# Five input buffers in place of two in the first stage of an attention and FFN block, their loads issued early

## The chip, the cores and the metric

The kernel runs on one core of one Trainium2 chip. The metric is the device time of one execution in microseconds (us). The engines are TensorE (PE), VectorE (DVE), ScalarE (ACT), GpSimd (POOL) and SyncE (SP), which here only issues DMAs.

## What is computed

A transformer block on x of 2 x 2048 x 256 (f32), with adaptive layer norms: a small conditioning vector c gives six modulations, and attention and a mixture of low-rank experts are added to x behind gates.

```python
mod = (_silu(L0_c) @ L0_wmod).reshape(L0_c.shape[0], 6, 1, -1)
sa, ca, ga, sb, cb, gb = (mod[:, 0], mod[:, 1], mod[:, 2], mod[:, 3], mod[:, 4], mod[:, 5])
...
h = _layernorm(x, axis=-1) * (1 + ca) + sa
x = x + ga * _L0_attn_ref(h, L0_attn_W_qkv, L0_attn_b_qkv, L0_attn_W_out, L0_attn_b_out)
h = _layernorm(x, axis=-1) * (1 + cb) + sb
x = x + gb * _L0_ffn_ref(h, ...)
```

The attention is causal, with 16 heads of 16. Inside it, the part that matters here is its beginning:

```python
qkv = x @ W_qkv.T + b_qkv
q, k, v = jnp.split(qkv, 3, axis=2)
```

## The kernel before

The 4096 rows of x (two sequences of 2048) are taken as 8 blocks of 512 (`NBLK`), each as 4 tiles of 128 rows. There are three stages. The first makes q, k and v of every block. The second is the attention, 8 groups of heads over 4 blocks of queries each. The third projects the result and does the FFN. Products are done in three passes of a high and a low half (`PASSES`, `product`), so each operand is split in two.

The first stage, for block n:

- SP loads the block into one of two buffers, `xs[:, n % 2]` (`load_x`, L429 to 431). Before it issues load n it waits until block n-2 has been rescaled by DVE (`xhat_done` at n-1), since that frees the buffer.
- DVE waits for the load and takes mean and variance (`moments`, L1191, which calls `statistics`, L409 to 412), ACT takes the root (`root`, L1058), and DVE writes `xhat` (`rescale`, L1195, which calls `standardise`, L416 to 423).
- PE turns `xhat` with 8 transposes (`turn`, L756, instructions at L761). ACT applies the modulation and makes the high half of `hT`, DVE the low half (`modulate`, L1062; `low`, L1198).
- PE projects q and k, 4 pieces of 6 matmuls of 512 columns (`project_qk`, L765, in `product` at L391), then v, 24 matmuls of 256 columns (`project_v`, L775).
- ACT moves the pieces of q and k to `parts[:, n % 2]` (`high`, L1072). Before it does, it waits until the stores of block n-2 out of the same buffer have landed (`parts_stored`). DVE makes the low half (`qk_low`, L1210). DVE moves v to `v_nat` (`v_rows`, L1217).
- SP stores `parts` to `qk_parts` in device memory, 4 DMAs of 512 KB (`store_parts`, L433 to 439), and from the round of block 1 on reads a block of the first head group back from there into `kst` and `qst`, 12 DMAs of 64 KB (`load_stacks`, L441 to 454).

The order on each engine is written out by hand. PE does, for n from 1 on, the turn of block n+1, then q and k and v of block n (L799 to 803). The q and k of block n wait until the low half of block n+1 is there and until DVE has taken the same piece of block n-1 out of PSUM (L767, L771). DVE does in round n: moments and rescale of block n+2, the low half of n+1, the four pieces of n, `v_nat` of n (L1251 to 1258). ACT does in round n: modulation of n+1, root of n+2, the pieces of n (L1090 to 1095). SP's loop, which the change touches, is L473 to 478:

```python
                load_x(2)
                for n in range(NBLK):
                    if n + 3 < NBLK:
                        load_x(n + 3)
                    store_parts(n)
                    if 1 <= n <= NJ:
                        load_stacks(0, n - 1)
```

SP executes this strictly in order. So load n+3 is issued after all of round n-1's stores and stack loads.

The attention's first work on PE is a fill of `ps` for the row maxima (`fill`, L832, matmuls at L863), which waits until `v_nat` of block 7 is written (`v_out`, L915). DVE reduces it to `mx` (L1266, L1270). POOL and ACT go on to the attention when all stores of `parts` have landed too (`first_stage_over`, L372): POOL then clears and fills `vw` (L633, L641), ACT does the exponentials (L1121).

Of the kernel before, what the change touches and what calls it, by code (L numbers as in the profile page):

```python
# [5 lines left out]
P = 128  # L6
# [7 lines left out]
B, S, D = 2, 2048, 256  # L14
# [7 lines left out]
KC, FC = D // P, FF // P  # L22
T = B * S
BLK = 512
TT = BLK // P
NBLK = T // BLK
# [19 lines left out]
LAST_OF_G = {g: max(LAST[u] for u in range(NU) if UNITS[u][0] == g) for g in range(NG)}  # L46
UNIT_AT_END = {LAST[u]: u for u in range(NU)}
PV_LAG, P_BUFS = 2, 4


def skip_of(n):
# [124 lines left out]
def until(eng, sem, count):  # L176
    if count > 0:
        eng.wait_ge(sem, count)


def build_program(nc, x, cT, wmod, wqkvT, bqkv, bv, woutT, bout, w1, b1, ar1, bl1, w2, b2, ar2, bl2, out):
# [4 lines left out]
    with ExitStack() as whole:  # L186
        def sem(name):
            return whole.enter_context(nc.semaphore(name))
# [4 lines left out]
        class Region:  # L193
# [50 lines left out]
        a = Region(rest_at)  # L244
# [12 lines left out]
        ar1_sb = a("ar1_sb", [P, KC, ZP])  # L257
        bl1_sb = a("bl1_sb", [LR, FF])
        bl2_sb = a("bl2_sb", [LR, D])
        xs = a("xs", [P, 2, TT, D])  # L260
        xhat = a("xhat", [P, TT, D])
        hf = a("hf", [P, KC, BLK])
        hT = a.pair("hT", [P, 2, KC, BLK])
# [1 line left out]
        stats = a("stats", [P, TT, 6])  # L265
        mv = a("mv", [P, TT, 2])
        rstd = a("rstd", [P, TT])
# [19 lines left out]
        f = Region(v_at)  # L287
# [10 lines left out]
        f = Region(bufs_at)  # L298
# [15 lines left out]
        xb_in = x.rearrange("(n t p) d -> n p t d", t=TT, p=P)  # L314
# [3 lines left out]


        c_in, wmod_in, wqkv_in, bias_in = sem("c_in"), sem("wmod_in"), sem("wqkv_in"), sem("bias_in")  # L320
        small_in, pad_in, x_in = sem("small_in"), sem("pad_in"), [sem(f"x_in{q}") for q in range(2)]
        consts, tables, padded, exp_c, silu_done = sem("consts"), sem("tables"), sem("padded"), sem("exp_c"), sem("silu_done")
        setup, w_hi, w_lo = sem("setup"), sem("w_hi"), sem("w_lo")
        small_hi, small_lo = sem("small_hi"), sem("small_lo")
# [2 lines left out]
        dve1, var_done, std_done, xhat_done, xT_done = (  # L327
            sem("dve1"), sem("var_done"), sem("std_done"), sem("xhat_done"), sem("xT_done"))
# [78 lines left out]
        def statistics(dve, link, xs, stats, mv, var_done):  # L407
            for t in range(TT):
                link(dve.bn_stats(stats[:, t, :], xs[:, t, :]), wait=(t == TT - 1))  # L409
            for t in range(TT - 1):  # L410
                link(dve.bn_aggr(mv[:, t, :], stats[:, t, :]), wait=False)
            dve.bn_aggr(mv[:, TT - 1, :], stats[:, TT - 1, :]).then_inc(var_done, 1)

        def standardise(dve, link, i, xs, mv, rstd, xhat, std_done, xhat_done, turned):
            until(dve, std_done, i + 1)
            link(dve.reciprocal(rstd[:], rstd[:]))  # L416
            until(dve, *turned)
            for t in range(TT):
                last = dve.tensor_scalar(xhat[:, t, :], xs[:, t, :], mv[:, t, 0:1], rstd[:, t:t + 1],  # L419
                                         ALU.subtract, ALU.mult)  # L420
                if t < TT - 1:
                    link(last, wait=False)
            last.then_inc(xhat_done, 1)

        with nc.Block() as block:
            @block.sync
            def _(sp):

                def load_x(n):  # L429
                    until(sp, xhat_done, n - 1)  # L430
                    sp.dma_start(xs[:, n % 2], xb_in[n]).then_inc(x_in[n % 2], 16)

                def store_parts(n):  # L433
                    for t in range(2):
                        sp.wait_ge(qk_lo, n * 2 * KC + (t + 1) * KC)
                        for h in range(2):
                            dst = qk_parts[t, h, :, n * BLK:(n + 1) * BLK]
                            sp.dma_start(dst.rearrange("(c p) t -> p c t", p=P),
                                         parts[:, n % 2, h, t * KC:(t + 1) * KC, :].bitcast(F32)).then_inc(parts_stored[n % 2], 16)

                def load_stacks(g, J, parts_of_load=ALL_PARTS):  # L441
                    c, hg, q = g // HG, g % HG, g % 2
                    n = c * NJ + J
                    sp.wait_ge(parts_stored[n % 2], 16 * 4 * (n // 2 + 1))
                    sp.wait_ge(ones_set[q], CLEARS)
                    cols = slice(n * BLK, (n + 1) * BLK)
                    for t, par in parts_of_load:
                        stack, order = (qst[q], (0, 0, 1)) if t == 0 else (kst[q], (0, 1, 0))
                        for row, h in enumerate(order):
                            src = qk_parts[t, h, hg * GH * HD:(hg + 1) * GH * HD, cols].rearrange(  # L450
                                "(p two r) t -> two r p t", two=2, r=HD)
                            at = par * STACK + row * HD
                            sp.dma_start(stack[at:at + HD, :, J * BLK:(J + 1) * BLK].bitcast(F32),  # L453
                                         src[par]).then_inc(kq_in[q][J], 16)

                sp.dma_start(c_sb[:], cT.rearrange("(k p) b -> p k b", p=P)).then_inc(c_in, 16)
                load_x(0)
                sp.dma_start(wmod_sb[:], wmod.rearrange("(k p) n -> p k n", p=P)).then_inc(wmod_in, 16)
                sp.dma_start(wqkv_sb[:], wqkvT.rearrange("(k p) n -> p k n", p=P)).then_inc(wqkv_in, 16)
                sp.dma_start(bq_sb[:], bqkv).then_inc(bias_in, 16)  # L460
                sp.dma_start(bv_sb[:], bv.broadcast_to((P, D))).then_inc(bias_in, 16)
                load_x(1)
                sp.dma_start(wout_sb[:], woutT.rearrange("(k p) n -> p k n", p=P)).then_inc(small_in, 16)
                sp.dma_start(b1_sb[:], b1).then_inc(small_in, 16)
# [4 lines left out]
                for r0 in (0, 32, 64):  # L469
                    sp.dma_start(bl1_sb[r0:r0 + ER], bl1).then_inc(pad_in, 16)  # L470
                    sp.dma_start(bl2_sb[r0:r0 + ER], bl2).then_inc(pad_in, 16)
                load_x(2)
                for n in range(NBLK):  # L473
                    if n + 3 < NBLK:
                        load_x(n + 3)
                    store_parts(n)
                    if 1 <= n <= NJ:
                        load_stacks(0, n - 1)
# [98 lines left out]
            def _(pool):  # L577
# [67 lines left out]
                def split_w(k):  # L645
                    pool.wait_ge(w_in, 16 * 3 * (k + 1))
                    width = KC * FF // W_PIECES
                    pieces = [(w1_p[0][:].rearrange("p k f -> p (k f)")[:, k * width:(k + 1) * width],
                               w1_p[1][:].rearrange("p k f -> p (k f)")[:, k * width:(k + 1) * width], w1_in[:]),
                              (w2_p[0][:, k, :], w2_p[1][:, k, :], w2_in[:])]  # L650
                    for hi, _, full in pieces:
                        pool.tensor_copy(hi, full).then_inc(ffn_hi, 1)
                    pool.wait_ge(ffn_hi, 2 * (k + 1))
                    for hi, lo, full in pieces:
                        pool.tensor_tensor(lo, full, hi.bitcast(F32), ALU.subtract).then_inc(ffn_lo, 1)
# [79 lines left out]
            def _(pe):  # L735
# [96 lines left out]
                def fill(e):  # L832
# [13 lines left out]
                    if ev[0] == "turn_x":  # L846
# [5 lines left out]
                        last.then_inc(fill_done, 1)  # L852
                        return
                    _, u, r, pairs, cb, width, on_diagonal = ev
                    g, J = UNITS[u]
                    q, k = qst[g % 2], kst[g % 2]
# [329 lines left out]
            def _(dve):  # L1186

                ready = Links(dve, setup)
                link1 = Links(dve, dve1)

                def moments(n):  # L1191
                    dve.wait_ge(x_in[n % 2], (n // 2 + 1) * 16)
                    statistics(dve, link1, xs[:, n % 2], stats, mv, var_done)

                def rescale(n):  # L1195
                    standardise(dve, link1, n, xs[:, n % 2], mv, rstd, xhat, std_done, xhat_done, (xT_done, n * KC))

                def low(n):  # L1198
                    dve.wait_ge(h_out, (n + 1) * 2 * KC)
# [44 lines left out]
                dve.wait_ge(bias_in, 32)  # L1244
                ready(dve.tensor_scalar(bq_sb[:, 0:KC], bq_sb[:, 0:KC], QSCALE, None, ALU.mult))
                moments(1)
                low(0)
                rescale(1)
# [12 lines left out]
                def maxima(e, ev):  # L1261
                    _, u, r, pairs, cb, width, _ = ev
                    bank = S_BANK + 2 * (e % 2)
                    dve.wait_ge(fill_done, e + 1)
                    if len(pairs) == 2:
                        dve.tensor_reduce(mx[:, u % 2, :, :, r, cb],  # L1266
                                          ps[:, bank:bank + 2, 0:2 * width].rearrange("p a (h x) -> p a h x", h=2),
                                          AX, ALU.max).then_inc(max_red, 1)
                    else:
                        dve.tensor_reduce(mx[:, u % 2, :, pairs[0], r, cb], ps[:, bank:bank + 2, 0:width],  # L1270
                                          AX, ALU.max).then_inc(max_red, 1)
# [223 lines left out]
```

## Time and profile before

| | us |
|---|---|
| median of 3 runs | 1308.25 |
| lowest and highest run | 1307.49, 1309.97 |
| the profiled execution's own time | 1304.39 |
| its span, first to last instruction | 1302.4 |
| PE busy | 1218.0 (94%) |
| DVE busy | 933.2 (72%) |
| ACT busy | 800.5 (61%) |
| POOL busy | 178.0 (14%) |
| mean granted clock of PE, share of full speed | 0.965 |

All rows further down are of the one profiled execution. Its times count from the start of the span. "L391" is line 391 of the kernel. An entry in brackets, as [4.50 <-DMA xs<-in_x], tells how long the engine was idle just before, and what ended it. SPq rows are issues of DMAs by the queue SP, and the time is that of the issuing, not of the transfer. PE's matmuls overlap, so their starts tell the pace, and not their durations. The first stage takes the first 109.77 us of the span, the attention most of the rest.

### The profile page before, as it was taken

To read this page: it belongs to the slowest core of one execution; us is meant where nothing else is said; L and a number is where in the kernel's file an instruction comes from. 1 tells how busy PE (TensorE), PEld (TensorE's weight loads), DVE (VectorE), ACT (ScalarE), POOL (GpSimd) and SP (SyncE) were. 2 spreads that over 40 slices of the span, in tenths; PEclk is the share of its full clock that TensorE was granted. 3 is DMA by queue.
4 is the path that set the end of the run, shared out by engine and by line. 5 is a ranking of instruction groups with operands and counts; after the bars stand their busy time and mean duration, and the time that the engine had idled before them with its cause. 6 is when DMAs were issued, how large, how long until landed. Compare 5 with 4: busy or idle time off the path is not lost.

```text
span 1302.4 us, 24602 instructions
## 1 busy us (share of the span) xinstructions
PE 1218.0 (94%) x9928; PEld 723.5 (56%) x9928; DVE 933.2 (72%) x1247; ACT 800.5 (61%) x1611; POOL 178.0 (14%) x153
## 2 busy tenths in 40 slices
PE   6988789999999999999999999999998899999997
PEld 5875334444444444444444444444444788898886
DVE  5877897888787887778887778786631576766553
ACT  4451466777777776767777667777675554444442
POOL 5205600000211000000000000200110132222310
PEclk9987798999999999999999999999899999999999
DMA  5793120031032021013003003500000222111100
GB/s 170 247 289 144 52 64 10 8 87 34 27 108 70 10 65 54 3 45 98 10 13 90 19 10 93 138 10 10 3 10 27 50 65 65 53 38 50 57 17 33
DMA packets 58121, 79.58 MB, mean 61 GB/s; under 512 B 12680, under 2 KB 28752, under 8 KB 58008
## 3 DMA queue, kind: packets, MB, share of 16 engines
q1 hardware_dynamic: 58008, 78.01, 20.3%
q8 instruction: 78, 1.28, 0.4%
q14 instruction: 35, 0.29, 0.1%
HBM read 47.57 MB, written 29.62 MB: 59 GB/s over the span
## 4 chain that ended last, share of the span: by engine, by line
PE 67%; DVE 12%; ACT 9%; issue 8%; SPq 2%; DMA 1%; POOL 0%; POOLq 0%; ACTq 0%; DVEq 0%
PE ps L907 21%; PE ps L882 17%; PE ps L863 9%; PE ps L391 8%; ACT prob L1121 7%; PE ps L1008 5%; DVE mx L1270 5%; PE ps L820 4%; PE ps L811 2%; DVE xhat L419 1%; DVE hid_lo L1413 1%; SPq L453 1%; ACT o_sb L1106 1%; DVE stats L409 1%; DMA wqkv_sb<-in_wqkvT 1%
## 5 line engine op out<-in xcount | busy, mean ns | idle before, releaser
L1121 ACT ACTIVATE prob<-ps 128x512 f32<-128x512 f32 (+3 forms) x1280 | 598.1, 537 | 263.0 <-PE ps L820 161.3
L1270 DVE TENSOR_REDUCE mx<-ps 128x2 f32<-128x1024 f32 (+1 forms) x512 | 594.0, 1188 | 148.2 <-PE ps L863 85.5
L882 PE MATMUL ps<-qst,kst 64*128 64x512 f32 (+3 forms) x1280 | 387.0, 446 | 18.9 <-ACT prob L1121 14.3
L882 PEld LDWEIGHTS ps<-qst,kst 64*128 64x128 f32 x1280 | 183.9, 188 | 270.2 <-ACT prob L1121 211.3
L907 PE MATMUL ps<-prob,vw 128*32 128x512 f32 (+3 forms) x3032 | 317.8, 492 | 3.4 <-ACT o_sb L1106 3.4
L863 PE MATMUL ps<-kst,qst 62*128 62x512 f32 (+3 forms) x1280 | 288.7, 425 | 21.5 <-DVE mx L1270 18.1
L863 PEld LDWEIGHTS ps<-kst,qst 62*128 62x128 f32 x1280 | 137.1, 193 | 95.4 <-DVE mx L1270 51.5
L907 PEld LDWEIGHTS ps<-prob,vw 128*32 128x32 f32 x3032 | 60.5, 108 | 86.9 <-issue 38.7
L820 PE MATMUL ps<-mask_kh,eye_h 64*128 64x128 bf16 x1024 | 99.6, 225 | 0.0
L1266 DVE TENSOR_REDUCE mx<-ps 128x4 f32<-128x512 f32 x64 | 60.9, 955 | 30.8 <-PE ps L811 30.4
L1413 DVE TENSOR_TENSOR hid_lo<-hidf,hid_hi 128x512 fp32r<-128x512 f32 x64 | 68.0, 1095 | 20.7 <-ACT hid_hi L1161 20.6
L1008 PE MATMUL ps<-w_hi,hid_hi 128*128 128x284 f32 x256 | 74.5, 315 | 5.3 <-ACT hid_hi L1161 5.3
L811 PE MATMUL ps<-mask_qh,eye_h 64*128 64x128 bf16 x1024 | 74.4, 225 | 0.0
L641 POOL COPY vw<-v_nat 128x1024 f32<-128x1024 f32 x8 | 8.3, 1039 | 469.3 <-PE ps L907 469.2
L1008 PE MATMUL ps<-w_lo,hid_hi 128*128 128x284 f32 x256 | 72.1, 306 | 0.0
L1161 ACT ACTIVATE hidf<-ps,b_sb 128x512 f32<-128x512 f32 x64 | 43.9, 686 | 37.7 <-PE ps L997 37.7
L1008 PEld LDWEIGHTS ps<-w_hi,hid_hi 128*128 128x128 f32 x256 | 51.0, 199 | 8.7 <-ACT hid_hi L1161 8.3
L391 PE MATMUL ps<-hT_hi,w_hi 128*128 128x512 f32 x128 | 52.4, 409 | 1.1 <-ACT hid_hi L1161 1.1
L820 PEld LDWEIGHTS ps<-mask_kh,eye_h 64*128 64x128 bf16 x1024 | 42.6, 97 | 17.1 <-issue 5.8
L1008 PEld LDWEIGHTS ps<-w_lo,hid_hi 128*128 128x128 f32 x256 | 51.3, 200 | 0.4
L1144 ACT ACTIVATE gexp<-gexp 128x12 f32<-128x12 f32 x16 | 3.4, 212 | 78.2 <-DVE gexp L1383 78.2
L391 PE MATMUL ps<-hT_hi,w_lo 128*128 128x512 f32 x128 | 50.9, 398 | 0.0
(157 smaller groups left out, 1350.5 us busy)
## 6 DMA issues: line engine op xcount, KB each, us to landing
qk_parts<-parts SPq DMA_DIRECT2D x32, 512.0 KB, 5.4
qst<-qk_parts SPq DMA_DIRECT2D x192, 64.0 KB, 2.4
kst<-qk_parts SPq DMA_DIRECT2D x192, 64.0 KB, 2.4
xs<-in_x SPq DMA_DIRECT2D x16, 512.0 KB, 8.4
o_all<-o_sb SPq DMA_DIRECT2D x32, 256.0 KB
o_raw<-o_all SPq DMA_DIRECT2D x16, 256.0 KB
rd<-rden_rows SPq DMA_DIRECT2D x16, 256.0 KB
out<-y SPq DMA_DIRECT2D x8, 512.0 KB, 3.2
```

The lines of the kernel that those rows point to most:

```text
L391: last = pe.matmul(out, lhs(i, k), rhs(j, k), start=(start and k == 0 and n == 0), stop=(stop and k == chunks - 1 and n == len(PASSES) - 1))
L811: last = pe.matmul(ps[:, bank + par, col:col + P], eye_h[rows, half, :], mask_qh[rows, half, :], start=False, stop=True, skip_group_check= ...
L820: last = pe.matmul(ps[:, L_BANK + (4 * n + h) % L_BUFS, 0:P], eye_h[rows, half, :], mask_kh[rows, half, :], start=False, stop=True, skip_g ...
L863: last = pe.matmul(ps[:, bank + par, at * width:(at + 1) * width], q[rows, p, J * BLK + r * P:J * BLK + (r + 1) * P], k[rows, p, cb * BLK: ...
L882: last = pe.matmul(ps[:, L_BANK + (4 * n + h) % L_BUFS, 0:BLK - skip], kst[g % 2][rows, h // 2, t * P:(t + 1) * P], qst[g % 2][rows, h // ...
L907: last = pe.matmul(ps[32 * h:32 * h + 32, O_BANK, skip + lo:skip + hi], vw[:, g % 2, t, h, :], prob[:, n % P_BUFS, h, lo:hi], start=(t == ...
L1008: last = pe.matmul(ps[:, Y_BANK + t, 0:D + ZP], hid[u][:, m, t * P:(t + 1) * P], w2_p[v][:, m, :], start=(e == 0), stop=(e == len(order) - 1))
L1121: act.activation(prob[:, n % P_BUFS, h, 0:width], ps[:, L_BANK + i % L_BUFS, 0:width], ACT.Exp).then_inc(exp_done, 1)
L1161: act.activation(dst, ps[:, H_BANK + m % 2, :], ACT.Relu, bias=b1_sb[:, m:m + 1]).then_inc(f1_out, 1)
L1266: dve.tensor_reduce(mx[:, u % 2, :, :, r, cb], ps[:, bank:bank + 2, 0:2 * width].rearrange("p a (h x) -> p a h x", h=2), AX, ALU.max).then ...
L1270: dve.tensor_reduce(mx[:, u % 2, :, pairs[0], r, cb], ps[:, bank:bank + 2, 0:width], AX, ALU.max).then_inc(max_red, 1)
L1413: dve.tensor_tensor(hid[1][:, m, :], hidf[:, m % HRING, :], hid[0][:, m, :].bitcast(F32), ALU.subtract).then_inc(hid_lo_done, 1)
```

## The change

`xs` gets five buffers instead of two, with a semaphore each. Load n waits until block n-5 has been rescaled. SP issues loads 2, 3 and 4 behind the small weights, where load 2 was alone, and in its loop load n+5 in place of load n+3: load 5 in round 0, load 6 in round 1, load 7 in round 2. Nothing is computed in another way, and the number of DMAs is the same.

```diff
+X_BUFS = 5
...
-        xs = a("xs", [P, 2, TT, D])
+        xs = a("xs", [P, X_BUFS, TT, D])
...
-        small_in, pad_in, x_in = sem("small_in"), sem("pad_in"), [sem(f"x_in{q}") for q in range(2)]
+        small_in, pad_in, x_in = sem("small_in"), sem("pad_in"), [sem(f"x_in{q}") for q in range(X_BUFS)]
...
                 def load_x(n):
-                    until(sp, xhat_done, n - 1)
-                    sp.dma_start(xs[:, n % 2], xb_in[n]).then_inc(x_in[n % 2], 16)
+                    until(sp, xhat_done, n - X_BUFS + 1)
+                    sp.dma_start(xs[:, n % X_BUFS], xb_in[n]).then_inc(x_in[n % X_BUFS], 16)
...
-                load_x(2)
+                for n in range(2, X_BUFS):
+                    load_x(n)
                 for n in range(NBLK):
-                    if n + 3 < NBLK:
-                        load_x(n + 3)
+                    if n + X_BUFS < NBLK:
+                        load_x(n + X_BUFS)
                     store_parts(n)
...
                 def moments(n):
-                    dve.wait_ge(x_in[n % 2], (n // 2 + 1) * 16)
-                    statistics(dve, link1, xs[:, n % 2], stats, mv, var_done)
+                    dve.wait_ge(x_in[n % X_BUFS], (n // X_BUFS + 1) * 16)
+                    statistics(dve, link1, xs[:, n % X_BUFS], stats, mv, var_done)
 
                 def rescale(n):
-                    standardise(dve, link1, n, xs[:, n % 2], mv, rstd, xhat, std_done, xhat_done, (xT_done, n * KC))
+                    standardise(dve, link1, n, xs[:, n % X_BUFS], mv, rstd, xhat, std_done, xhat_done, (xT_done, n * KC))
```

## Rows read from the trace of the kernel before

**Rows 1.** Windows: length; busy us of PE, PEld, DVE, ACT, POOL; clock; DMA share; GB/s.
```profile
60.00:70.00 10.00, 7.50 (x47) 6.43 (x47) 8.25 (x19) 5.40 (x9) 0.00 (x0) 1.00 1.01 289
...
80.00:90.00 10.00, 10.00 (x45) 8.38 (x44) 5.94 (x17) 3.66 (x7) 0.00 (x0) 0.74 0.98 304
```

**Rows 2.** Waits, 0 to 125 us, DVE: total us, times, longest.
```profile
DVE stats L409 <- DMA xs<-in_x: 13.5, 5, 4.5
```

**Rows 3.** Timeline of DVE: start, duration, line, operation, count, idle before.
```profile
47.78 1.39 DVE L409 BATCH_NORM_STATS2 stats<-xs 128x6 f32<-128x256 f32 x4
...
55.23 1.22 DVE L1219 TENSOR_TENSOR v_nat<-ps,bv_sb 128x1024 f32<-128x1024 f32 x1
60.95 1.40 DVE L409 BATCH_NORM_STATS2 stats<-xs 128x6 f32<-128x256 f32 x4 [4.50 <-DMA xs<-in_x]
```

**Rows 4.** Timeline of PE: turns (L761), first and last matmuls (L391), first fill (L863).
```profile
44.25 1.03 PE L761 MATMUL ps<-ident,xhat 128*128 128x128 f32 x8
...
53.58 1.03 PE L761 MATMUL ps<-ident,xhat 128*128 128x128 f32 x8
...
64.78 1.09 PE L761 MATMUL ps<-ident,xhat 128*128 128x128 f32 x8 [1.71 <-DVE xhat L419]
...
77.14 1.09 PE L761 MATMUL ps<-ident,xhat 128*128 128x128 f32 x8 [1.77 <-DVE xhat L419]
79.02 0.76 PE L391 MATMUL ps<-hT_hi,wqkv_hi 128*128 128x512 f32 x1 [0.79 <-DVE parts L1213]
...
85.41 0.39 PE L391 MATMUL ps<-hT_hi,wqkv_hi 128*128 128x512 f32 x1
...
90.35 1.03 PE L761 MATMUL ps<-ident,xhat 128*128 128x128 f32 x8
...
99.82 0.40 PE L391 MATMUL ps<-hT_hi,wqkv_hi 128*128 128x512 f32 x1
...
105.43 0.28 PE L391 MATMUL ps<-wqkv_hi,hT_hi 128*128 128x256 f32 x1
...
109.77 0.44 PE L863 MATMUL ps<-kst,qst 62*128 62x128 f32 x4 [1.36 <-issue]
```

**Rows 5.** Timeline of the queue SP: issues of stores, loads and stack loads.
```profile
34.22 2.88 SPq L438 DMA_DIRECT2D qk_parts<-parts  x4
...
56.42 0.42 SPq L431 DMA_DIRECT2D xs<-in_x  x1
...
67.81 0.42 SPq L431 DMA_DIRECT2D xs<-in_x  x1
...
79.09 0.41 SPq L431 DMA_DIRECT2D xs<-in_x  x1
...
86.46 2.75 SPq L453 DMA_DIRECT2D kst<-qk_parts  x6
```

**Rows 6.** Windows (columns as in Rows 1), cut where the kind of transfer changes.
```profile
18.00:34.00 16.00, 14.80 (x65) 12.28 (x66) 9.95 (x22) 6.35 (x11) 13.68 (x15) 1.00 0.13 39
...
60.80:66.20 5.40, 3.37 (x28) 2.93 (x26) 4.82 (x15) 2.84 (x6) 0.00 (x0) 1.00 1.05 391
66.20:72.50 6.30, 5.83 (x26) 4.76 (x27) 3.43 (x5) 2.56 (x4) 0.00 (x0) 1.00 0.92 181
...
90.60:93.50 2.90, 2.90 (x17) 2.34 (x16) 2.90 (x5) 2.52 (x4) 0.00 (x0) 1.00 0.82 169
```

**Rows 7.** Timelines of ACT and of POOL.
```profile
87.67 2.40 ACT L1076 ACTIVATE parts<-ps,bq_sb 128x512 fp32r<-128x512 f32 x4
...
126.83 1.28 ACT L1121 ACT_TABLE_LOAD   x1 [20.51 <-PE ps L820]
...
111.58 1.81 POOL L633 MEMSET vw<- 128x2048 f32 x1 [68.78 <-DMA qk_parts<-parts]
```

**Rows 8.** Window (columns as in Rows 1) in which the clock is at half.
```profile
113.00:130.00 17.00, 12.94 (x77) 7.04 (x73) 15.01 (x18) 2.63 (x4) 16.01 (x18) 0.51 0.01 2
```

**Rows 9.** The page: granted clock in tenths, 40 slices of 32.6 us.
```profile
PEclk9987798999999999999999999999899999999999
```

## The prediction

> **What bounds the kernel now.** First the busy table by stretch, for the stage that the change touches [rows 1]: from 60 to 70 us TensorE (PE) is busy for 7.50 of 10 us, its clock falls to a mean of 0.74 in 80 to 90, and the DMA engines are busy at 0.98 to 1.01 of their time in both. Three things could set the pace, and the shares don't say which. Next the waits of VectorE (DVE) [rows 2]: 13.5 us in 5 pieces for `xs`. The timelines put this in order. DVE's statistics of block 5 start at 60.95, after 4.50 us of waiting for the load; those of blocks 6 and 7 are two more such rows, with 3.66 and 3.62 us [rows 3]. PE follows: its turns of blocks 5 and 6 start after waits of 1.71 and 1.77 us for `xhat`, and the projection behind the second waits 0.79 us more (a like row stands behind the first) [rows 4]. The queue SP shows why the loads are late: load 5 is issued at 56.42, load 6 at 67.81, load 7 at 79.09 [rows 5]. Each comes behind the stores and the 12 small stack loads of the round before. It is not a taken buffer that holds them: load 5 needs block 3 rescaled, and by 47.78 DVE is already at the statistics of block 4 [rows 3].
>
> How fast would PE go without these waits? Turns at 44.25 and 53.58 give 9.33 us a block [rows 4]. DVE's own block of work, from 47.78 to the end of `v_nat` at 56.45, is 8.67 us, less than that [rows 3]. From the turn at 53.58 the next ones come after 11.20, 12.36 and 13.21 us, and the last block's first matmul (it has no turn) 9.47 us after that, where 9.33 each is possible: 1.87 + 3.03 + 3.88 + 0.14 = 8.92 us [rows 4]. Of the 3.88, most is the clock. Fifteen matmuls of 512 columns fill 79.02 to 85.41, 0.426 us each (the 1.2 GHz level); the last block's 24 fill 99.82 to 105.43, 0.234 each (2.4 GHz). That is 15 x 0.192 = 2.9 us [rows 4]. What PE did before this fall were the waits just named.
>
> **The change, part by part.** (a) Loads 2 to 5 are now issued one behind the other, where load 2 was. All small transfers are issued ahead of them as before, SP has nothing else until the first store at 34.22 [rows 5], and the DMA engines are busy at 0.13 from 18 to 34 us [rows 6]. The three loads that come forward, 0.52 MB each, take 1.3 us each at the 391 GB/s of a full stretch [rows 6]. Cost: 0, since that idle time hides them; without it 3.9 us, on whatever small load came behind, and none does. (b) Load 6 takes the place that load 4 had, right after the first store, load 7 that of load 5, 56.42. DVE will ask for block 7 at about 74, so all three late waits (4.50 + 3.66 + 3.62 = 11.8 us) go. They don't count in full: PE is next, and only its 8.92 count. Until 56.42 no wait changes, so the saving begins there. (c) SP loses the issues at 67.81 and 79.09, 0.42 us each [rows 5]. (d) The loads' waits for `xhat` look back further and are met when SP comes to them; more semaphores and a larger tile add no instruction: 0.
>
> What is late next? With PE at 9.33 us a block, the projections of blocks 4 to 7 begin at 63.7, 73.0, 82.4 and 91.0. PE ends its last block 8.9 us before the 108.41 of now, at 99.5, and the attention's first fill, which waits for the last `v_nat` (1.36 us), comes at 100.9 instead of 109.77 [rows 4]. DVE keeps up, by its 8.67. The other that must is the queue: `parts` has two buffers, so ScalarE (ACT) writes block n+2 only when the store of block n has landed. SP's rounds begin at 56.42, 67.81 and 79.09, 11.39 and 11.28 us apart, longer than 9.33 [rows 5]. Unhindered, six stack loads are issued in 2.75 us [rows 5], 0.46 each, so a round of 17 issues is about 8 us of SP's own; the rest is waiting for room in the DMA queues. These need 5.4 us for a store, 6.3 for stacks and an input load, and 2.9 for stacks alone where all were queued in time [rows 6]. Taking the load away gives between 1.3 us (its bytes at 391 GB/s) and 3.4 (6.3 less 2.9). So a round of 11.3 becomes 7.9 to 10.0 us if the DMA engines pace it, and 10.9 if SP's issuing does. The store of block 2 is through at about 66.2 [rows 6]; that of block 5, for which ACT's last block waits, at 66.2 + 3 rounds. Behind it come 2.4 us of ACT [rows 7] and 0.7 of DVE, and then `v_nat`. That meets PE's 99.5 at a round of 10.0. I take 9.8, nearest to the measured 11.3 less the load's bytes: hidden, by half a microsecond. At 10.9 the stage ends 2.8 us later.
>
> Behind the stage, GpSimd clears `vw` when the last store has landed, at 111.58, for 1.81 us, and ACT's first work of the attention is at 126.83 [rows 7]. The store shifts less than PE, by some 5 to 8 us, and this cover of 13 us shrinks by up to 4 and stays. All later stages do the same work in the same order, so they shift whole.
>
> One rule speaks against the change. In 60 to 90 us the DMA share is about 1.0 [rows 1]. The Trainium skill (Perfetto Trace Analysis, "What "DMA-bound" means") says that where the DMA engines or the issuing sequencer bind, large descriptors are what matters; loading ahead only moves bytes. By it the rounds keep their pace, which is the first rival below.
>
> **The sum.** 1.87 + 3.03 + 3.88 + 0.14 = 8.9 us. The profiled run took 1304.39 us (span 1302.4) and becomes 1295.5. The median of the three runs, 1308.25, is 3.86 above the profiled one; with the saving taken from the median: 1299.3.
>
> **The rivals.**
> First, the queue takes the place of the load. For it: rounds of 11.3 us at a DMA share near 1.0. Against it: 3 us of a round is waiting for room, which the removed bytes give back. At a round of 10.9 the stage ends 2.8 us later than forecast, 6.1 saved: 1302.2.
>
> Second, the clock. If its fall inside the stage comes anyway, the 2.9 us stay: 1302.2. For it: the rows don't say what starts a fall, and another lasts from 113 to 130 [rows 8]. Against it: none is there up to 78, where PE has hardly a gap, and after the change it has none to 99. The other way, if 113 to 130 were spent less at half clock, PE's 12.94 busy us there could shrink [rows 8], of which DVE lets pass a part; I allow 3 us. The Trainium skill (TensorE: Matmul & The Clock Gate, "HAM oscillation") reckons the loss as throttled time times a half: 3.2 us for the 6.4 seen, where the starts of the matmuls give 2.9.
>
> Third, the gain is swallowed before the end: the attention starts on the last store, by `vw`, and not on `v_nat`. Against it: 13 us of cover. It gives 1306 to 1309.
>
> Fourth, slower. All of the attention now starts 8.9 us earlier against the clock's changes, and a fall can come where PE sets the pace. From 163 us on the page's clock is at 9 tenths nearly throughout [rows 9]; a microsecond at half clock there costs half a microsecond. It takes (8.9 + 2.6) x 2 = 23 us more of it before the kernel is slower by 0.2%; the longest in the rows is 17 [rows 8]. With 30 us more: 1299.3 + 15 = 1314.
>
> **How the numbers follow.** Forecast, 8 to 9.5 us saved, and with it what the clock may give beyond: 0.62. Queue 0.15, clock fall kept 0.10, swallowed 0.09, slower 0.04. 0.2%, 2.6 us, is about what a measurement of this kernel can tell from no change. Faster: 0.62 + 0.15 + 0.10 = 0.87; same 0.09; slower 0.04. The range runs from 3 us of clock beyond the forecast, with the 0.8 by which the lowest run lies under the median, to the queue's and the clock's 1302.2 with the 1.7 of the highest above it: 1295.5 to 1304.
>
> **What would show it.** Right: no wait of DVE for `xs` after block 1, turns 9.33 us apart from 44 us on, full clock to 99, the first fill near 100.9, SP's rounds under 10 us. The queue rival: ACT's pieces of `parts` waiting for the stores of two blocks before, and `v_nat` waiting for them. The clock rival: a stretch at half clock before 100. Swallowed: ACT's first work of the attention not 9 us earlier. The prediction is wrong if the first fill comes at 101 and the span is not 9 us shorter; the loss would then lie behind the stage.

## The result

| | before | after |
|---|---|---|
| median of 6 runs, us | 1307.3 (1305.43 to 1309.97) | 1299.57 (1295.65 to 1302.93) |
| the profiled execution's own time | 1304.39 | 1297.24 |
| its span | 1302.4 | 1295.3 |
| its first fill of the attention | 109.77 | 103.36 |

The ratio of after to before is 0.994, interval 0.9922 to 0.9958, or 5.5 to 10.2 us saved. A later measurement of the same kernel, `after_again` below, gives 0.9944 (0.9922 to 0.9966). The forecast was 1299.3. A ratio is the time of a kernel over that of the kernel before, measured beside it; the numbers in brackets behind a ratio are its 95% interval, those behind a median in the table the lowest and the highest run.

The forecast named the stage's end as the place where the saving is made, and there it was too large: the first fill came 6.4 us earlier, not 8.9. What it said of the loads and of PE came out. What it said of the queue did not, and the queue rival is what happened. (A round is one pass of SP's loop: a store of `parts` in four DMAs, and 12 stack loads.) First the engines between 60 and 90 us, in the columns of [rows 1]:

```profile
60.00:70.00 10.00, 10.00 (x63) 8.85 (x62) 9.56 (x22) 6.20 (x11) 0.00 (x0) 1.00 0.96 308
70.00:80.00 10.00, 10.00 (x64) 8.90 (x63) 9.55 (x23) 5.88 (x10) 0.00 (x0) 1.00 0.84 273
80.00:90.00 10.00, 10.00 (x64) 8.89 (x63) 6.47 (x9) 5.23 (x8) 0.00 (x0) 1.00 0.87 285
```

PE is busy for all of it at full clock. Before, it was busy for 7.50 of the first 10 us, and its clock was 0.74 in the last 10 [rows 1]. The statistics of blocks 5 to 7 follow one another without any wait for a load, where the first of them waited 4.50 us [rows 3]. DVE's timeline:

```profile
56.60 1.39 DVE L410 BATCH_NORM_STATS2 stats<-xs 128x6 f32<-128x256 f32 x4
...
65.19 1.39 DVE L410 BATCH_NORM_STATS2 stats<-xs 128x6 f32<-128x256 f32 x4
...
73.79 1.39 DVE L410 BATCH_NORM_STATS2 stats<-xs 128x6 f32<-128x256 f32 x4
...
99.40 2.73 DVE L1215 SCALAR_TENSOR_TENSOR parts<-ps,bq_sb,parts 128x512 fp32r<-128x512 f32 x4 [6.96 <-ACT parts L1078]
102.04 1.22 DVE L1221 TENSOR_TENSOR v_nat<-ps,bv_sb 128x1024 f32<-128x1024 f32 x1
```

The last two lines are the new thing: DVE stands 6.96 us for ACT before the last block, and its last `v_nat` starts at 102.04. PE's timeline (turns, first fill), against [rows 4], and ACT's:

```profile
62.99 1.03 PE L763 MATMUL ps<-ident,xhat 128*128 128x128 f32 x8
...
72.33 1.03 PE L763 MATMUL ps<-ident,xhat 128*128 128x128 f32 x8
...
81.66 1.03 PE L763 MATMUL ps<-ident,xhat 128*128 128x128 f32 x8
...
103.36 0.69 PE L865 MATMUL ps<-kst,qst 62*128 62x128 f32 x4 [3.75 <-issue]
```
```profile
86.59 2.45 ACT L1078 ACTIVATE parts<-ps,bq_sb 128x512 fp32r<-128x512 f32 x4 [1.50 <-DMA qk_parts<-parts]
98.68 2.42 ACT L1078 ACTIVATE parts<-ps,bq_sb 128x512 fp32r<-128x512 f32 x4 [9.64 <-DMA qk_parts<-parts]
121.29 1.28 ACT L1123 ACT_TABLE_LOAD   x1 [20.19 <-PE ps L822]
```

The turns are 9.34 and 9.33 us apart. PE ends its projections at 103.36 - 3.75 = 99.61; forecast was 99.5. Then it stands 3.75 us in place of 1.36. It waits for the last `v_nat`; DVE writes that behind its pieces of `parts`, those come behind ACT's, and ACT waited 9.64 us for the store of block 5 to land. The reason is in SP's rounds, to be compared with [rows 5]:

```profile
57.06 3.90 SPq L439 DMA_DIRECT2D qk_parts<-parts  x4
61.06 4.28 SPq L454 DMA_DIRECT2D qst<-qk_parts  x6
65.38 2.75 SPq L454 DMA_DIRECT2D kst<-qk_parts  x6
68.18 3.06 SPq L439 DMA_DIRECT2D qk_parts<-parts  x4
71.34 5.12 SPq L454 DMA_DIRECT2D qst<-qk_parts  x6
76.51 3.02 SPq L454 DMA_DIRECT2D kst<-qk_parts  x6
79.57 3.11 SPq L439 DMA_DIRECT2D qk_parts<-parts  x4
...
89.80 13.91 SPq L439 DMA_DIRECT2D qk_parts<-parts  x12
```

From store to store the rounds take 11.12, 11.39 and 10.23 us, against 11.39 and 11.28 before. In the second there is no input load any more, and it is not shorter. Windows of the same execution show why a load's bytes were no cost there (columns as in [rows 1]):

```profile
60.00:66.00 6.00, 6.00 (x44) 5.54 (x43) 6.00 (x11) 3.43 (x6) 0.00 (x0) 1.00 1.06 399
66.00:68.00 2.00, 2.00 (x10) 1.63 (x9) 1.56 (x9) 1.38 (x4) 0.00 (x0) 1.00 0.70 131
76.00:80.00 4.00, 4.00 (x23) 3.43 (x22) 3.96 (x9) 2.48 (x4) 0.00 (x0) 1.00 0.59 134
```

While stores run, the window has 399 GB/s; while stack loads run, 131 to 134 GB/s with the DMA engines 0.59 to 0.70 busy. SP issues six stack loads of 64 KB in 2.75 us, 0.46 us each, which is 142 GB/s: in these stretches it is SP's issuing that sets the rate, and the DMA engines had room for an input load.

### The profile page after: what moved, and what is told of

Its sections match the earlier page's. It is cut to its first block, busy times and chain, and to the rows that moved or that the text cites. A ratio compares the mean times of both kernels' runs of the same rounds, so it can differ in the third digit from the quotient of the medians.

```text
span 1295.3 us, 24602 instructions
## 1 busy us (share of the span) xinstructions
PE 1216.4 (94%) x9928; PEld 725.0 (56%) x9928; DVE 931.2 (72%) x1247; ACT 800.0 (62%) x1611; POOL 178.1 (14%) x153
## 4 chain that ended last, share of the span: by engine, by line
PE 72%; DVE 10%; ACT 9%; issue 8%; DMA 1%; POOL 0%; SPq 0%; POOLq 0%; ACTq 0%; DVEq 0%
PE ps L909 21%; PE ps L884 17%; PE ps L392 11%; PE ps L865 9%; ACT prob L1123 7%; PE ps L1010 5%; DVE mx L1272 5%; PE ps L822 4%; PE ps L813 2%; DVE hid_lo L1415 1%; ACT o_sb L1108 1%; DMA wqkv_sb<-in_wqkvT 1%; DVE stats L410 1%; DVE xhat L420 1%; DVE x L1320 1%
```

## The experiments

Each kernel was timed beside the kernel before the change. Its profile is of one execution.

**Buffers or place.** Two kernels take the change apart. The first has the five buffers and leaves the issues where they were:

```diff
-                for n in range(2, X_BUFS):
-                    load_x(n)
+                load_x(2)
                 for n in range(NBLK):
-                    if n + X_BUFS < NBLK:
-                        load_x(n + X_BUFS)
+                    if n + 3 < NBLK:
+                        load_x(n + 3)
```

> Five buffers, but load n+3 issued in round n as before the change. If the place of the issue is what counts: DVE waits 4.50, 3.66 and 3.62 us for blocks 5 to 7 as before, the first fill comes near 109.8 us and the time is that of before (1307) within 2 us. If the waits for a free buffer counted: those waits go, first fill near 103.4, and the time is that of the changed kernel (about 1299.6).

Ratio 1.0011 (0.9993 to 1.0028). DVE's waits for `xs` from 36 to 112 us (total, times, longest) and the first fill:

```profile
DVE stats L410 <- DMA xs<-in_x: 11.5, 3, 4.3
```
```profile
109.80 0.44 PE L864 MATMUL ps<-kst,qst 62*128 62x128 f32 x4 [1.36 <-issue]
```

The second is the kernel before with its two buffers, and each load one round earlier:

```diff
                 load_x(2)
+                load_x(3)
                 for n in range(NBLK):
-                    if n + 3 < NBLK:
-                        load_x(n + 3)
+                    if n + 4 < NBLK:
+                        load_x(n + 4)
```

> Two buffers as before, load n+4 issued in round n (loads 2 and 3 ahead of the loop), so loads 5, 6 and 7 go out at about 43, 56.4 and 68 us. If the place of the issue counts: no wait of DVE above 1 us after block 1 (block 7's load lands near 73.5, DVE asks at 73.8), first fill near 103.4, time as the changed kernel's, about 1300. If the number of buffers counted: waits of 3 us or more for blocks 5 to 7, and about 1305 to 1307.

Ratio 0.9955 (0.9939 to 0.9971), median 1300.75. The first fill, and ACT's waits for stores in the stage:

```profile
102.85 0.44 PE L864 MATMUL ps<-kst,qst 62*128 62x128 f32 x4 [3.42 <-issue]
```
```profile
ACT parts L1077 <- DMA qk_parts<-parts: 14.5, 3, 8.1
```

So three more buffers alone give nothing, and the earlier place with two buffers gives the whole effect within the measurement. The extra buffers only allow a freer choice of place, and the kernel needs one round.

**What held the stage's end.** The changed kernel with a third buffer of `parts`, laid over the input weights, which are used up when block 2 needs it (the cut shows the count, ACT's wait and ACT's write; SP's and DVE's uses go with them):

```diff
+PART_BUFS = 3
...
-                    until(act, parts_stored[n % 2], n // 2 * 16 * 4)
+                    until(act, parts_stored[n % PART_BUFS], n // PART_BUFS * 16 * 4)
...
-                        act.activation(parts[:, n % 2, 0, c, :], ps[:, QK_BANK + c, :], ACT.Identity,
+                        act.activation(part(n)[0][:, part(n)[1], 0, c, :], ps[:, QK_BANK + c, :], ACT.Identity,
```

> The changed kernel with three buffers of parts (the third lies over weights that are used up), so ACT waits for the store of block n-3 instead of n-2. In the changed kernel ACT's last block waited 9.64 us for a store and the first fill 3.75 us behind PE. If that wait costs what the stage lost against the forecast: ACT's last block starts near 92.5, the last v_nat is done near 100.8, first fill near 101, 2.4 us earlier than the changed kernel; time about 1297. If something else held v_nat (DVE's own work, or PE): first fill stays at 103.4 and the time at 1299.6.

```profile
100.65 0.44 PE L872 MATMUL ps<-kst,qst 62*128 62x128 f32 x4 [1.36 <-issue]
```

The first fill is at 100.65, where the forecast had 100.9, and the wait before it is the old 1.36. SP's rounds are as long as before (stores at 56.74, 68.06, 79.47, 89.83). So the two buffers of `parts` passed the length of the rounds on, and that cost 2.7 us at the stage's end. The median is 1299.7, ratio 0.9943 (0.9921 to 0.9965): the 2.7 us don't show in it. More on this below.

The same third buffer in the kernel before:

> The kernel before the change with three buffers of parts. If the stores held nothing up before the change: DVE still waits 11.8 us for blocks 5 to 7, first fill at 109.8, time that of before within 2 us. If the stores already cost something beside the loads: first fill 2 to 3 us earlier and 1304 to 1305.

```profile
DVE stats L416 <- DMA xs<-in_x: 12.9, 3, 4.6
```
```profile
111.92 0.33 PE L870 MATMUL ps<-kst,qst 62*128 62x128 f32 x2 [1.36 <-issue]
```

The waits are of 36 to 112 us. Ratio 1.0015 (0.9996 to 1.0034), so the third buffer gains nothing here: as long as the loads came late, the stores held nothing up. The fill is 2 us later than before. DVE's statistics of block 7 start at 86.74, 1.1 us later than before, and the profile has two falls of the clock in the stage, mean 0.79 in 64 to 72 and again in 88 to 96; whether the third buffer has a part in this stays open.

**What makes a round long.** The stack loads with a quarter of their bytes. This kernel leaves out three quarters of the first head group's q and k, so its results are not those of the reference; it serves for the first stage's timeline only:

```diff
+                    width = BLK // 4 if g == 0 else BLK
...
-                            sp.dma_start(stack[at:at + HD, :, J * BLK:(J + 1) * BLK].bitcast(F32),
-                                         src[par]).then_inc(kq_in[q][J], 16)
+                            sp.dma_start(stack[at:at + HD, :, J * BLK:J * BLK + width].bitcast(F32),
+                                         src[par, :, :, 0:width]).then_inc(kq_in[q][J], 16)
```

> The changed kernel, but the 48 stack loads of the first stage carry 128 columns each instead of 512 (the rest of the stacks is constants, so the attention of the first head group computes on part of its data only). Same number of issues, a quarter of their bytes (0.2 MB a round instead of 0.8). SP's rounds were 11.1 and 11.4 us in the changed kernel, though the input load was gone from the second. If a round is the drain of a store (5.4 us, in which SP stands still) and then SP's own issuing of the stack loads at 0.46 us each: rounds of 10.5 to 11.4 us, and ACT's last block still waits over 7 us for a store. If bytes set the round: under 10 us, and that wait is under 6 us.

It was executed once, which gives no ratio; two clearings of the stacks that it adds at the start make its whole stage some 3 us later. SP's timeline, and a window in which only stack loads run:

```profile
59.91 3.60 SPq L439 DMA_DIRECT2D qk_parts<-parts  x4
...
70.71 2.94 SPq L439 DMA_DIRECT2D qk_parts<-parts  x4
...
81.88 2.94 SPq L439 DMA_DIRECT2D qk_parts<-parts  x4
...
92.06 13.32 SPq L439 DMA_DIRECT2D qk_parts<-parts  x12
```
```profile
77.00:81.00 4.00, 4.00 (x19) 3.22 (x18) 3.54 (x14) 3.48 (x7) 0.00 (x0) 1.00 0.15 36
```

Rounds of 10.80, 11.17 and 10.18 us with 0.6 MB less in each, and ACT still waits 8.34 us. The DMA engines are busy for 0.15 of their time in that window, while SP issues one load after the other: behind the store it is SP's issuing alone that holds the round. The bytes alone don't make the round. Now the other way, the same bytes in fewer issues:

```diff
+WIDE = 2
...
-                    if 1 <= n <= NJ:
-                        load_stacks(0, n - 1)
+                    if 1 <= n <= NJ and n % WIDE == 0:
+                        load_first_stacks(n - WIDE)
```

> The changed kernel with the stack loads of the first stage taken for two blocks at once: 24 DMAs of 128 KB in place of 48 of 64 KB, the same bytes. If SP's issuing sets the pace of the stores: the store of block 5 is issued near 84 instead of 89.8, ACT's last block starts near 92.5 without a wait, first fill near 101 instead of 103.4, and the clearing of vw starts near 104 instead of 109.4; about 2 us less than the changed kernel, 1297 to 1298. If the bytes set it: the store of block 5 is still issued at 89 or later, first fill 103, time unchanged.

> As wide2, with all four blocks at once: 12 DMAs of 256 KB in the round of block 4. By SP's issuing: stores of blocks 2, 3 and 4 go out at once when DVE is done, near 55.5, 64 and 72.7; the 3.1 MB of stacks take some 8 us behind the store of block 4, so the store of block 5 lands near 93; first fill near 101 to 102, vw near 104. By bytes: the same bytes in one piece, first fill at 103 or later.

Neither half of what I expected of `wide2` came whole. The store of block 5 was indeed issued at 84.12, yet ACT waited 9.06 us for it, the first fill came at 102.79 and `vw` at 108.77, not 104. Ratio 0.9929 (0.9904 to 0.9955), which doesn't tell it from the changed kernel. Two windows in which its stack loads run:

```profile
66.00:70.00 4.00, 4.00 (x21) 3.32 (x20) 3.56 (x12) 2.77 (x6) 0.00 (x0) 1.00 1.07 138
84.00:88.00 4.00, 4.00 (x19) 3.22 (x18) 2.85 (x4) 2.95 (x5) 0.00 (x0) 1.00 1.04 166
```

Here the loads are all issued, the DMA engines are busy throughout, and they move 138 and 166 GB/s; why the second is faster stays open.

`wide4` is slower than the kernel before, 1.0037 (1.0011 to 1.0064), median 1312.12. A window of it while the stack loads run, and ACT:

```profile
80.00:98.00 18.00, 18.00 (x108) 15.82 (x107) 6.77 (x8) 5.32 (x8) 0.00 (x0) 1.00 1.02 129
```
```profile
107.08 2.42 ACT L1097 ACTIVATE parts<-ps,bq_sb 128x512 fp32r<-128x512 f32 x4 [19.09 <-DMA qk_parts<-parts]
```

All twelve loads, 3.1 MB, are issued by 80.37, and the store of block 5 right behind them. They pass at 129 GB/s for more than 18 us, and the store with them in front has to wait. My expectation of 8 us for them was off by a factor of three. Each of these loads writes 16 partitions, a store reads 128. That they are reads of device memory is not what makes them slow: input loads read it too and write 128 partitions, and from 18 to 21 us, where only they run, the changed kernel moves 383 GB/s. The Trainium skill (SBUF — State Buffer, "Door 1: The DMA port swizzle") says that the rate of a DMA follows from how many of 16 ports its partitions reach, and that 16 adjacent ones reach 4, 104 to 109 GB/s. The traces agree in kind, and measure more: 129 in `wide4`, 138 and 166 in `wide2`. No run here varies the number of partitions, so that it is the cause is argued, not shown.

So a block's stack loads cost SP 12 x 0.46 = 5.5 us of issuing, and the DMA engines between 0.79 MB / 166 GB/s = 4.7 us and 0.79 MB / 129 GB/s = 6.1 us (an estimate, by the rates of `wide2` and `wide4`). The two run side by side and are about equal, which is why taking away either leaves the round nearly as it is. A round is then roughly the drain of the store, 5.4 us, in which SP's issuing is slowed (the first ten issues of the round from 57.06 take 8.3 us, the last six 2.75), plus one of these.

> Three buffers of parts and the wide stack loads together. Both act on the same wait of ACT for a store, so together they give what one gives: first fill near 100.7, as with three buffers alone, and not 5 us less than the changed kernel. What is different from three buffers alone is only the end of the stores, vw near 104 instead of 109.1; if anything waits for that behind the stage it shows in the time, else about 1297 to 1299.

First fill 100.83, no wait of ACT for a store; ratio 0.9926 (0.9899 to 0.9953). As expected, the two act on one wait. The other half was wrong: `vw` comes at 109.30 and not near 104, so the stores don't end earlier.

**Out of the stores' way.** The changed kernel with the stack loads of blocks 2 and 3 behind the last store:

```diff
-                    if 1 <= n <= NJ:
+                    if 1 <= n <= NJ // 2:
                         load_stacks(0, n - 1)
+                for J in range(NJ // 2, NJ):
+                    load_stacks(0, J)
```

> The changed kernel with the stack loads of blocks 2 and 3 issued behind the last store instead of between the stores, still two buffers of parts. What stood between the stores in the queue was the stack loads, some 6 us a block by SP's issuing (0.46 us each) and as much by the DMA engines (131 GB/s into 16 partitions). So the stores of blocks 3 to 6 go out when DVE is done with them, ACT's last block starts near 92.4 without a wait, first fill 100.8, vw near 103.5 to 104. By the rival, that the drain of the stores alone holds ACT up: ACT's last block still waits and first fill stays above 102.

```profile
ACT parts L1080 <- DMA qk_parts<-parts: 0.6, 1, 0.6
```
```profile
101.14 0.44 PE L867 MATMUL ps<-kst,qst 62*128 62x128 f32 x4 [1.36 <-issue]
```
```profile
103.16 1.81 POOL L637 MEMSET vw<- 128x2048 f32 x1 [60.17 <-DMA qk_parts<-parts]
```

ACT's waits are down to 0.6 us with two buffers of `parts`; the fill comes at 101.14 and `vw` at 103.16. So it was what stood between the stores, and not their own drain. The median is 1295.89, ratio 0.9911 (0.9888 to 0.9933), the lowest of all here.

Or all stack loads from GpSimd's queue (a semaphore of its own, `kq_pool`, goes with it):

```diff
-                    if 1 <= n <= NJ:
-                        load_stacks(0, n - 1)
...
+                            pool.dma_start(stack[at:at + HD, :, J * BLK:(J + 1) * BLK].bitcast(F32),
+                                         src[par]).then_inc(kq_pool[J], 16)
```

> The changed kernel with all stack loads of the first stage issued by GpSimd, which is idle from 44 to 109 us, so that SP issues stores and input loads alone. By the queue theory SP's stores go out when DVE is done with them, ACT never waits, first fill 100.8. By the bytes (the DMA engines are shared, 131 GB/s for the stack loads wherever they are issued) the stores are slowed beside them and land later: first fill between 101 and 103.4.

```profile
100.81 0.44 PE L885 MATMUL ps<-kst,qst 62*128 62x128 f32 x4 [1.36 <-issue]
```
```profile
60.00:84.00 24.00, 24.00 (x152) 21.50 (x151) 21.54 (x45) 13.75 (x23) 13.28 (x27) 1.00 1.00 318
```

First fill 100.81, ACT waits for no store, ratio 0.9928 (0.9908 to 0.9949). Stores and stack loads now pass together, 318 GB/s from 60 to 84 us. That is 7.6 MB, some 2.3 of them stack loads; one kind after the other, at 400 GB/s and at 129 to 166, they would take 27 to 31 us in place of 24 (an estimate). So a stack load holds a store up where it stands ahead of it in the same queue, and much less from another queue.

**Whether the stage's end is the kernel's end.** The changed kernel and `parts3` once more, beside the last two, all four on one chip:

> The changed kernel once more, beside the three below on one chip. First fill at 103.4; median 1299 to 1301. It is what the others are compared with.

> Three buffers of parts once more. Its stage ended 2.7 us earlier than the changed kernel's, its median did not. If the missing part was the clock's falls, which come differently from run to run: over more runs a median 1 to 3 us below after_again's. If something behind the stage takes the 2.7 us back each time: the same median as after_again.

| | first fill, us | median, us | ratio to before |
|---|---|---|---|
| `after_again` | 102.70 | 1301.38 | 0.9944 (0.9922 to 0.9966) |
| `parts3_again` | 100.82 | 1300.2 | 0.9937 (0.9912 to 0.9962) |
| `pool_stacks` | 100.81 | 1298.51 | 0.9928 (0.9908 to 0.9949) |
| `late_stacks` | 101.14 | 1295.89 | 0.9911 (0.9888 to 0.9933) |

All four intervals overlap, and 12 runs of `parts3_again` went from 1292.03 to 1307.49. The 2 us of the stage are too little to be told from this spread. One pair seems to stand out: five of the six runs of `late_stacks` lie under the lowest of `after_again` (1298.58), and its median is 5.5 us lower, where its fill is 1.6 us earlier. But its mean clocks are higher too, 0.961 to 0.969 against 0.960 to 0.964, and time follows clock: of the 12 runs of `parts3_again`, the three near 1292 have 0.970 and 0.971, the two at 1307 have 0.956. One line through the 165 runs of 13 kernels whose mean clock is on record, with a level for each kernel, has a slope of 8.8 us for 0.01 of mean clock, and the runs scatter about it by 1.1 us. At one clock, 0.962, the levels are (an estimate):

| kernel | us at 0.962 |
|---|---|
| before | 1307.8 |
| changed, its two measurements | 1301.4 and 1300.9 |
| `parts3`, `parts3_again` | 1300.7 and 1300.8 |
| `late_stacks` | 1299.8 |
| `pool_stacks` | 1299.8 |

So the change saves 6.5 to 7.0 us at equal clock, which is what the first fill gained (6.4 and 7.1). Most of the 5.5 us of `late_stacks` is its clock; some 1 us is left, no more than the levels of six runs can be off. Which of the four is best is not settled beyond their being faster than before.

Where the spread comes from, two traces show in one stretch, 925 to 1040 us, the end of the attention and the first block of the last stage. `parts3`, then before:

```profile
925.00:1040.00 115.00, 108.14 (x771) 64.89 (x772) 38.11 (x63) 65.40 (x135) 10.98 (x5) 0.81 0.08 25
```
```profile
925.00:1040.00 115.00, 103.65 (x820) 60.89 (x816) 43.30 (x71) 71.86 (x145) 10.96 (x5) 0.91 0.09 25
```

Mean clock 0.81 against 0.91: (0.91 - 0.81) x 115 x 2 = 23 us more at half clock. The copy of `o_sb` that is at 894.99 in before is at 886.62 in `parts3`, 8.4 us earlier, of the stage's 9.1. It is not the attention's last copy, which is at 1004.35 in before. The copy at 976.68 in before is still 8.6 us earlier, at 968.08. But ACT's table load of the last stage, at 1024.98 in before, is at 1023.90, 1.1 earlier, and the span ended 1301.3 against 1302.4, again 1.1 earlier. So the gain came nearly whole through most of the attention and was lost within 50 us around the attention's end, where PE is busy nearly all the time and the clock is what differs between the two. It goes the other way too: in the changed kernel the first of these copies is at 887.25, 7.7 us earlier, the second at 965.55, 11.1 earlier, and the span ends 7.1 earlier, of the stage's 6.4. That the clock is the cause is read from these traces and from the line through the runs; no run sets the clock.

## Why the prediction was right, and where not

- **The waits for `xs` go, and PE is next.** Right. No wait after block 1, turns 9.33 us apart, PE's work of the stage done at 99.61 against a forecast of 99.5.
- **The loads were late for their place in the queue and not for a buffer.** Right, and shown by the two halves of the change: 1.0011 for the buffers, 0.9955 for the place.
- **The moved loads cost nothing.** Nothing late was seen before 56 us; the first projections and stores are where they were within a microsecond.
- **The clock's fall inside the stage goes.** Right in this profile (1.00 from 60 to 90). But counting 2.9 of the 3.88 us to it was a misreading. In `bufs_only` the fall came at another place, mean clock 0.79 in 64 to 72 and full from 72 to 110, and the stage ended at the same 109.80. There DVE's statistics of block 7 start at 85.62, as before (85.60), and PE stood for them instead (the turn at 89.46 waits 1.44 us, the projection behind it 0.79). So load 7 set the end of the stage before the change, and the slow stretch was hidden under its lateness. The sum of 8.92 us is not touched by this, its split is. For the clock rival the prediction also says that PE had hardly a gap up to 78; [rows 1] has it busy for 7.50 of 10 us from 60 to 70, at full clock.
- **SP's round becomes 9.8 us.** Wrong, and this is the term that was mis-sized. I took 1.3 us for the load's bytes from an 11.3 us round, and 0.2 more for which I gave no reason: by the bytes alone the round is 10.0, where the working has no margin left. The round with no load took 11.39, the next 10.23. The step that failed is "the rest is waiting for room in the DMA queues", with the conclusion that removed bytes give it back. The waiting is the store's drain. The stack loads behind it are no faster for the load's absence, since SP's issuing (`thin_stacks`) and their own slow passage through the queue (`wide2`, `wide4`) bound them, each by itself. The row that misled was 2.9 us for "stacks alone" in 90.6 to 93.5 [rows 6]: 2.9 us at 169 GB/s are 0.5 MB, the rest of a block of stack loads that had begun to drain before, and not the whole of 0.79 MB; 181 GB/s at 66.2 to 72.5 in the same group was nearer the truth.
- **Hidden by half a microsecond.** Wrong for the same reason. The rival's formula was right, the store of block 5 at 66.2 + 3 rounds: with the measured rounds, 32.7 us for the three, that is 98.9, and ACT begins at 98.68, and the fill comes 2.5 us later than forecast. The rival had put it at 2.8 later and had a chance of 0.15. With a margin of 0.5 us on a guessed round it deserved about as much as the forecast.
- **The cover of `vw` and ACT.** Held: `vw` at 109.38, ACT's first work of the attention at 121.29, 5.5 us earlier. That is 0.9 us less than the fill's 6.4. The clock fell near 101.9, while PE stood, and the first fills ran at half clock, where `parts3` kept full clock over the same time and has both 9.1 us earlier. In `parts3_again`, with a mean clock of 0.54 from 102 to 104, the fill is 8.95 us earlier and ACT's first work, at 118.51, 8.3. In windows of after and of `parts3`:

```profile
102.00:104.00 2.00, 0.64 (x8) 0.67 (x10) 1.26 (x2) 0.00 (x0) 0.00 (x0) 0.50 1.05 406
```
```profile
102.00:104.00 2.00, 1.15 (x12) 0.60 (x12) 2.00 (x4) 0.00 (x0) 0.00 (x0) 1.00 1.05 408
```

- **The total.** 1299.3 against 1299.57 is luck in good part. The working gives 8.9 us; the stage gave 6.4, which is the queue rival's 6.1 and not the forecast's 8 to 9.5, and the two measurements gave 7.7 and 5.6 by their medians. The forecast also started from 1308.25, the median of three runs, where six runs of the same kernel gave 1307.3: the start was 1 us too high and the saving 1.2 us larger than measured, and the two cancel. At equal clock the change saved 6.5 and 7.0 us, so the 7.7 has about 1 us of clock in it, too.

## What to carry to other kernels

When a load comes late, look first at what stands ahead of it in its queue; more buffers don't move an issue, and one place further up the program did all of this change's work. Before a freed transfer is counted as time, find what bounds the stretch it lay in: a queue can be full by the time its issues take, while its DMA engines have room (0.15 to 0.70 busy here), or by transfers that pass slowly and hold up what stands behind them. When the next limit is within half a microsecond of the one removed, give both outcomes the same chance.

## What the runs showed that was not expected

- Queued loads that write 16 partitions pass at 129 GB/s (`wide4`) to 166 GB/s (`wide2`), stores out of 128 at about 400, and a store queued behind them waits: 19.09 us of ACT in `wide4`. The busy share of the DMA engines does not tell the two apart, 1.02 at 129 GB/s and 1.06 at 399.
- From another queue the same loads pass beside the stores: 318 GB/s together in `pool_stacks`, and no wait of ACT.
- SP's issues of 64 KB and of 16 KB take the same 0.46 us each (six in 2.75), and 128 KB as well. At 0.46 us, 129 to 166 GB/s are 59 to 76 KB, so the two limits of a stack load are about equal just at 64 KB.
- Changes of 2 to 3 us in one stage can't be read from medians of 6 to 12 runs here. The first fill's time in a trace tells them at once: 102.70 to 103.36 for the changed kernel, 100.65 to 101.14 for the five in which ACT's wait is gone or down to 0.6 us. Setting each run beside its own mean clock takes most of the spread away, from 15 us between runs of one kernel to a scatter of 1.1.
